# One of VectorE's two one-hot blocks per edge group is built by GpSimd

## What is computed

```python
y = cond_layer_norm(x, cond, ...)                 # four layers of this
scores = einsum('ehd,ehd->eh', q[src], k[dst])    # 4 heads of 128
attn   = softmax of scores over the edges of one src
x = x + segment_sum(attn * v[dst], src) @ wo + bo
x = x + relu(cond_layer_norm(x) @ m_w1 + m_b1) @ m_w2 + m_b2
...
x = layernorm(x + layers(x))
x = layernorm(x + segment_sum(x[dst] * edge_weight, src) @ weight.T)
```

## Time and profile before

| what | value |
|---|---|
| runs of the kernel before | 2155.28, 2156.07, 2156.99 us |
| profiled execution, span from first to last instruction | 2156.0 us |
| stage of the edge tables in it | from about 69 to 235 us |
| VectorE busy in the whole span | 1331.7 us (62%) |
| TensorE busy in the whole span | 1915.0 us (89%) |
| GpSimd busy in the whole span | 550.8 us (26%) |

### The profile page before, as it was taken

One profiled execution on the slowest core, in us unless ns is written; L12 is line 12 of the kernel. 1 busy time (PEld: TensorE's weight loads), 2 busy tenths in 40 slices (PEclk: granted clock), 3 DMA queues, 4 the chain that ended last, 5 costly groups with the idle time before them and its releaser, 6 DMA issues.

```text
span 2156.0 us, 38976 instructions
## 1 busy us (share of the span) xinstructions
PE 1915.0 (89%) x14203; PEld 1710.9 (79%) x14203; DVE 1331.7 (62%) x2487; ACT 929.3 (43%) x1566; POOL 550.8 (26%) x589
## 2 busy tenths in 40 slices
PE   1566399999989899999998999999989999998998
PEld 0455289898978789989787899898878988987777
DVE  8899956556574565564846646557555565566654
ACT  1798434444343253443533434444334344444221
POOL 5222312212153121121432212213422121224301
PEclk9999699999999999999999999999999999999999
DMA  1200300000010000000100000000100000002112
GB/s 22 84 0 0 146 11 16 11 11 21 6 41 5 25 16 6 16 16 11 32 13 25 11 11 16 11 11 16 34 25 11 6 21 11 11 6 97 37 63 69
DMA packets 43311, 53.81 MB, mean 25 GB/s; under 512 B 2929, under 2 KB 29342, under 8 KB 43129
## 3 DMA queue, kind: packets, MB, share of 16 engines
q1 hardware_dynamic: 43136, 51.46, 7.7%
HBM read 40.58 MB, written 10.62 MB: 24 GB/s over the span
## 4 chain that ended last, share of the span: by engine, by line
PE 68%; DVE 12%; issue 11%; POOL 4%; ACT 3%; DVEq 2%; DMA 1%; ACTq 0%; POOLq 0%
PE ps L1202 61%; PE ps L1380 5%; POOL prob L501 3%; ACT prob L634 1%; DVEq L869 1%; PE ps L1311 1%; DVE y L972 1%; DVE CW L880 1%; DVE prob L1001 1%; ACT v_hi L628 1%; DVE v_lo L991 1%; DVE CW L883 1%; DVE y L965 1%; DVE yT_lo L977 1%; DVE L L927 1%
## 5 line engine op out<-in xcount | busy, mean ns | idle before, releaser
L501 POOL TENSOR_SCALAR prob<-prob,rnorm 128x1250 f32<-128x1250 f32 x160 | 211.3, 1320 | 1006.8 <-DVE rnorm L1009 1006.8
L1017 DVE TENSOR_TENSOR PT_lo<-ps,PT_hi 128x512 fp32r<-128x512 f32 x400 | 275.4, 689 | 39.4 <-ACT PT_hi L643 19.6
L643 ACT ACTIVATE PT_hi<-ps 128x512 fp32r<-128x512 f32 x400 | 237.2, 593 | 84.4 <-PE ps L1380 72.9
L1380 PE MATMUL ps<-ident,prob 128*128 128x128 f32 x1600 | 244.4, 275 | 30.2 <-POOL prob L501 28.3
L634 ACT ACTIVATE prob<-prob,nmax 128x1250 f32<-128x1250 f32 x160 | 214.1, 1338 | 126.0 <-DVE nmax L1001 126.0
L1001 DVE CUSTOM_DVE_ANT_0 prob<-ps,L 128x1250 f32<-128x1250 f32 x160 | 232.3, 1452 | 22.3 <-PE ps L1202 20.8
L1202 PE MATMUL ps<-PT_hi,v_hi 128*128 128x256 f32 x800 | 237.6, 297 | 6.8 <-DVE v_lo L991 6.2
L1380 PEld LDWEIGHTS ps<-ident,prob 128*128 128x128 f32 x1600 | 186.2, 141 | 56.2 <-issue 29.4
L1202 PE MATMUL ps<-PT_hi,v_lo 128*128 128x256 f32 x800 | 226.2, 283 | 0.0
L1202 PE MATMUL ps<-PT_lo,v_hi 128*128 128x256 f32 x800 | 226.1, 283 | 0.0
L1202 PE MATMUL ps<-k_hi,q_hi 128*128 128x512 f32 (+2 forms) x480 | 187.0, 390 | 1.5 <-DVE nmax L1001 1.5
(11 more groups left out here) (202 smaller groups left out, 4722.4 us busy)
## 6 DMA issues: line engine op xcount, KB each, us to landing
piece<-in_L_gnn_m_w_dram SPq DMA_DIRECT2D x32, 256.0 KB, 2.7
w_table<-CW SPq DMA_DIRECT2D x1, 6250.0 KB, 17.1
prob<-w_table SPq DMA_DIRECT2D x10, 625.0 KB, 4.1
x<-in_x_dram SPq DMA_DIRECT2D x2, 2304.0 KB
piece<-in_L_gnn_wq_dram SPq DMA_DIRECT2D x16, 256.0 KB, 2.8
piece<-in_L_gnn_wk_dram SPq DMA_DIRECT2D x16, 256.0 KB, 3.0
piece<-in_L_gnn_wv_dram SPq DMA_DIRECT2D x16, 256.0 KB, 2.8
piece<-in_L_gnn_wo_dram SPq DMA_DIRECT2D x16, 256.0 KB, 2.6
```

Of the source, the lines that this page charges most:

```text
L501: pool.tensor_scalar(buf, buf, r, 1.0, ALU.mult, ALU.mult).then_inc(S["probs_ready"], 1)
L643: act.activation(o, i, ACT.Copy).then_inc(S["pt_hi"], 1)
L1017: dve.tensor_tensor(lo, i, hi.bitcast(F32), ALU.subtract).then_inc(S["pt_split"], 1)
L1380: m = pe.transpose(bank(5 + n % 2, at * P, (at + 1) * P), prob[:, (NT * h + 2 * g + j) % 3, d * P:(d + 1) * P], ident[:])
```

## The change

GpSimd makes block 1 of every group, VectorE keeps block 0, ScalarE block 2. The sources of eight groups are copied into a small tile `psrc` once per pass of the loop, since a GpSimd instruction here takes its scalar from a fixed place. TensorE waits for one more semaphore, `p_onehot`. VectorE also makes three one-hots fewer ahead of its loop.

```diff
+            psrc = sb("psrc", [P, UNROLL_G], F32, edges)
...
@@ GpSimd
                 with pool.Fori(0, NCH // 2) as i:
+                    pool.wait_ge(p_onehot, START + i * UNROLL_G)
+                    pool.sem_inc(pool_passed, 1)
+                    pool.tensor_copy(psrc[:], eT[:, 0, 1, bass.ds(i * UNROLL_G, UNROLL_G)]).then_inc(p_src, 1)
+                    pool.wait_ge(p_src, START + i + 1)
                     for c in range(2):
                         pool.wait_ge(e_win, i * 2 + c + 1)
...
                         m.then_inc(e_parts, 1)
+                        for gl in range(CHUNK_G):
+                            j = c * CHUNK_G + gl
+                            pool.wait_ge(e_sum, START + i * UNROLL_G + j - AHEAD)
+                            pool.sem_inc(pool_passed, 1)
+                            pool.tensor_scalar(onehot[:, j % SBUFS, 1, :], iota_h[:], psrc[:, j:j + 1], None, ALU.is_equal)\
+                                .then_inc(p_onehot, 1)
@@ VectorE
             def sources(j, b, group):
                 m = dve.tensor_scalar(onehot[:, j % SBUFS, b, :], iota_h[:], eT[:, 0, b, group], None, ALU.is_equal)
-                if b == GK - 2:
-                    m.then_inc(e_onehot, 1)
+                m.then_inc(e_onehot, 1)
...
                 for j in range(AHEAD):
-                    for b in range(GK - 1):
-                        sources(j, b, slice(j, j + 1))
+                    sources(j, 0, slice(j, j + 1))
...
                         dve.tensor_tensor(only, only, sums[:, 2], ALU.add).then_inc(e_chain, 1)
-                        sources(j + AHEAD, 1, ahead)
                         dve.wait_ge(e_chain, at + 2)
@@ TensorE
                         pe.wait_ge(a_onehot, START + i * UNROLL_G + j + 1)
+                        pe.wait_ge(p_onehot, START + i * UNROLL_G + j + 1)
```

More of the change, by code:

```diff
@@ L243, in build @@
         flag_read = sem("flag_read")
-        a_dist, a_onehot = sem("a_dist"), sem("a_onehot")
+        a_dist, a_onehot, p_onehot, p_src = sem("a_dist"), sem("a_onehot"), sem("p_onehot"), sem("p_src")
         e_win, e_parts, e_onehot, e_sum, e_added, e_chain = (sem(n) for n in ("e_win", "e_parts", "e_onehot", "e_sum", "e_added", "e_chain"))
@@ L256, in build @@
         stored = [sem(f"stored{i}") for i in range(2)]
-        counted = [*S.values(), e_sum, e_chain, g_chain, a_dist, a_onehot]
+        counted = [*S.values(), e_sum, e_chain, g_chain, a_dist, a_onehot, p_onehot, p_src]
         def t_bank(n):
```

## The result

The changed kernel takes 2247.04 us (median of 4, 2244.59 to 2247.77) against 2155.68 for the kernel before on the same chip: a ratio of 1.042, 95% interval 1.041 to 1.043, or 91 us slower. Forecast were 2175.5 and a range up to 2195. The sign was right; the size was wrong by more than four times.

The account below looks back on a forecast made before the run. VectorE was taken to bound the table stage, its 2.70 us step set by a chain through the register load. Terms -6 + 20.5 + 2.6 + 2.4 = +19.5 us on 2156.0 gave 2175.5 us; forecast 2164 to 2185, range 2156 to 2195.

Parts of the forecast that it names:

- The bound and the shadow: Table stage: VectorE sets the pace; its second one-hot runs beside the register load and adds nothing to an ordinary step.
- The load chain: VectorE's loop: register load and address work, 1.02 us from the second add's end, keep an ordinary step at 2.70 us.
- credit of 6: VectorE's loop: removing 56 second one-hots and their conflicts gains 0.85 us in each of 7 passes, -6 us.
- The mutual stop: Shared ports: a VectorE one-hot stands still for as long as GpSimd's instruction runs, and the reverse; adds into `CW` don't.
- rival B: GpSimd's tensor_scalar does not stop VectorE, so only the credit is left: 2150 us, chance 0.08.
- The step that failed: Duration of each of GpSimd's 56 new one-hots, scaled from L501 to 1280 elements: 1.35 us, bounds 1.20 and 2.5.
- Rival A: GpSimd itself becomes the stage's bound because its one-hot is slow, about 2.5 us; chance 0.13.
- The sign that it named: In the stage, TensorE would wait for GpSimd's one-hots and the window products would come late.
- The conflict's price: VectorE's remaining one-hot L841 waits 0.37 us on average for GpSimd, 56 times: +20.5 us, ends 10 to 27.
- The random phase: L841 meets GpSimd at random, GpSimd at work 0.62 of the time with 0.59 us left: mean wait 0.37 us.
- The start: Ahead of the loop, VectorE's preparations wait for GpSimd's first one-hots, delaying TensorE's start: +2.4 us (0 to 4).
- The windows: VectorE's window instruction L835 meets GpSimd: 14 waits of 0.37 us, half hidden, +2.6 us (0 to 5).

Follow-up runs that it names:

- 860 columns: The changed kernel with GpSimd's one-hot compare cut to 860 of 1280 columns, rest of block 1 left out: 2177.32 us (2155.89 before), ratio 1.010.
- at 1.33 us: The changed kernel with GpSimd's compare replaced by two multiplications over all 1280 columns, block 1 left zero: 2164.04 us (2156.59 before), ratio 1.004.
- the run with 460 columns: The changed kernel with GpSimd's one-hot compare cut to 460 of 1280 columns, rest of block 1 left out: 2154.75 us (2157.25 before), ratio 0.999.

## Why the prediction was wrong

- **The bound and the shadow: right.** The load chain, not the second one-hot, set the step. Taking the one-hot away gave 4.1 us (credit of 6 forecast; by its own terms, 8 x 2.88 less 22.3, it is 0.74 a pass and 5.2 in all, not 0.85 and 6), taking the chain away as well 14.
- **The mutual stop: right**, for tensor_scalar too; rival B is out. All 38 delayed one-hots of the loop end 0.35 us after GpSimd. The Trainium skill ("SBUF — State Buffer", Who interferes with whom) calls the shared ports an exclusive lock, held for the whole instruction. At 1280 columns VectorE's one-hots agree; at 460 and 860 columns they end up to 0.44 and 1.12 us before GpSimd does, and there the measurement decides.
- **The step that failed: "L501, one tensor in, one scalar, ... scaled to 1280 it is 1.35 us, which I take".** It measured 3.5 alone and 3.7 in the stage. I matched the operation's name, its inputs and width, but not its arithmetic: L501 is two multiplications, and that pair is a fast case. The step is a mis-sized term: the duration of one GpSimd one-hot, from which the overlap (at work 0.62 of the time) and the bound followed. My upper bound of 2.5 us, from a two-input subtraction, was under it too, so the range could not hold the result. Of the 91.4 us some 84 come from this step: with the duration that I took 7.5 are left.
- **Rival A was the right mechanism** with 13%, and its duration of 2.4 us was still too short; near that (2.42 us, 860 columns) 21 us were measured where it priced 33, though at a cut width some of VectorE's one-hots slip in. Its cause was wrong: a multiplication takes as long as a compare. The sign that it named did not show either: the waits did not move to the new semaphore, as told below. The Trainium skill ("GPSIMD Engine Reference") gives 2.03 cycles an element for a compare that is not unrolled (Performance pitfalls for Q7 kernels) and a clock of 1.2 GHz (Specifications); the estimate from these is 1.7 ns a column. The runs show 2.56, and show it for a multiplication as well.
- **The conflict's price: too high.** +20.5 us forecast (0.37 us per one-hot); at the duration that I took it is 56 x 0.13 = 7 us. The random phase was wrong: I had seen that a one-hot waiting for `e_sum` is done before VectorE asks, and kept the average all the same. At the duration that I took the result is +7.5, at the very edge of my 2164 to 2185. The four measured terms, -4.1, +7, +3 and nothing for the windows, sum to 6.
- **The start: +2.4 forecast**, +3.0 at 1.33 us (first add at 76.7 instead of 73.7, up to 0.5 of it that run's own clearing of a column, behind which GpSimd's first one-hot starts at 62.8 instead of 62.3), +7.3 in the changed kernel (81.0), again by the duration.
- **The windows: +2.6 forecast**, none at 1.33 us (L848 stays at 0.55), 1.8 us each in the changed kernel. So a VectorE instruction that reads two SBUF tensors stops too: the window takes 2.50 us behind a running one-hot of GpSimd.

Why do the waits name L891 (78.8 us of TensorE's waiting) and the new semaphore only 17.2 us, when GpSimd is the bound? In most groups VectorE stands in L852 or L846 behind GpSimd, and TensorE behind VectorE's add, so the last wait that TensorE sees is VectorE's. The bound shows where nobody is waited for: GpSimd idles 9.0 us in the stage, and the chain that ended last runs through L478.

## What to carry to other kernels

Before moving an instruction to another engine, look for a row of the same arithmetic there, not only of the same name and shape; where none exists, an appended run of a few forms settles it in one execution. What an engine would gain must be read from the chain between two steps: 0.55 us of busy time taken from the busiest engine was worth 0.07 us a group, since a register load ran beside it. And an engine that shares ports is not free because it is idle: one 3.5 us instruction in every four groups cost 33 us.

## What the runs showed that was not expected

- GpSimd's one-input instructions of 1280 columns: 3.5 us with one operation (compare or multiplication, in float16, bf16 and float32); 1.33 with mult-mult or, in float32, mult-add; 4.6 with a compare and a second operation; 1.25 for a copy.
- The stop is not always for the whole of GpSimd's instruction. In the run with 460 columns VectorE's one-hots that met one ended 0.44 us before it did (0.55 to 0.70 us long, GpSimd's 1.42), with 860 columns up to 1.12 us before; at 1280 none did. With 860 columns the place within GpSimd's instruction decides: one-hots that came in its first 0.73 us ended 1.32 us after its start, those that came after 1.05 to 1.5 us took their usual 0.55, and those that came after 1.8 to 2.1 us ended 0.35 behind its end. So it does not hold VectorE off all the time; why is open. For the same reason the 460-column run understates the conflict: it stands 2.5 us under the kernel before, the full-width one of nearly equal duration 7.5 above it.
- TensorE's granted clock in the stage was 0.80 of 2.4 GHz in the mean (1.00 before), so it stood at the lower level (1.2 GHz) for part of it: 1.00 from 77 to 100 us, 0.67 from 100 to 120. Ahead of the fall, from 86 to 103 us, the engine did a group's matmuls in 1.85 us and then stood idle for 1.7 to 2.7. At the lower level a group's 30 matmuls took 3.38 us. That this cost nothing is only argued, from GpSimd's 9 us of idle time; no run held the clock up.
